# The order and the number in flight of eight weight loads on SyncE's queue, in a state-space mixer followed by an MLP

## The reference

```
x = x + mixer(layernorm(x))
x = x + mlp(layernorm(x))
mixer: proj = h @ W_in * mup; z, xBC, dt = split(proj); xBC = silu(conv4(xBC))
       dt = softplus(dt + bias); dA = exp(dt * -exp(A_log))
       state = state * dA + (dt * x) B;  y = state C + D * x
       g = y * silu(z); g = g * rsqrt(mean(g^2)) * norm_w; out = g @ W_out
mlp:   down(silu(gate(h) * gate_s) * (up(h) * up_s)) * down_s, 512 -> 1408 -> 512
```

## Time and profile before

| what | value |
|---|---|
| time before, median of 3 runs | 766.48 us |
| the three runs | 766.48, 765.35, 768.88 us |
| the profiled execution, its own time | 770.17 us |
| its span, first to last instruction | 768.5 us |
| mean granted TensorE clock | 0.99 |
| PE busy | 735.6 us, 96% of the span |
| DVE, ACT, POOL busy | 513.3, 492.6, 292.2 us |

### The profile page before, as it was taken

The page is one execution under the profiler, slowest core; times in us unless marked ns, Lnnn a source line. Parts: engine busy times, 40 slices in busy tenths (PEclk is TensorE's granted clock), DMA queues, the critical chain, the costliest instruction groups (busy, mean ns, idle before and its releaser), DMA issues.

```text
span 768.5 us, 20313 instructions
## 1 busy us (share of the span) xinstructions
PE 735.6 (96%) x8486; PEld 609.4 (79%) x8486; DVE 513.3 (67%) x845; ACT 492.6 (64%) x933; POOL 292.2 (38%) x235
## 2 busy tenths in 40 slices
PE   4878999999999999999999998989999999999997
PEld 4866778888887887887887886778888888888886
DVE  5977876987987897797797796763624532632331
ACT  6998978978978978979879878624312321321330
POOL 2055276366456547637617707630021011002002
PEclk9988999999999999999999999999999999999999
DMA  9831444484485286366376389535122013002002
GB/s 296 241 93 28 95 112 112 99 243 126 85 243 139 81 210 170 84 160 202 84 210 191 81 227 312 189 99 163 42 70 96 0 42 123 0 16 94 0 1 85
DMA packets 42300, 94.97 MB, mean 124 GB/s; under 512 B 9889, under 2 KB 15777, under 8 KB 42017
## 3 DMA queue, kind: packets, MB, share of 16 engines
q1 hardware_dynamic: 42208, 93.67, 42.8%
HBM read 84.73 MB, written 17.57 MB: 133 GB/s over the span
## 4 chain that ended last, share of the span: by engine, by line
PE 84%; ACT 8%; DVE 4%; issue 2%; DMA 1%; POOL 0%; SPq 0%; ACTq 0%; DVEq 0%; POOLq 0%
PE ps_y L1742 10%; PE ps_proj L1729 10%; PE ps_proj L1271 8%; PE ps_proj L1272 8%; PE ps_proj L1273 8%; PE ps_out L1729 6%; PE ps_x L1729 6%; PE ps_y L1347 5%; PE ps_x L1358 4%; PE ps_out L1371 4%; PE ps_out L1372 3%; PE ps_out L1373 3%; PE ps_x L1324 3%; ACT ring L721 2%; ACT ring L725 2%
## 5 line engine op out<-in xcount | busy, mean ns | idle before, releaser
L532 POOL TENSOR_TENSOR ring<-tokd,ring 128x1024 f32<-128x1024 f32 x64 | 122.3, 1926 | 175.7 <-ACT tokd L716 130.9
L1271 PE MATMUL ps_proj<-xn_hi,win_x_hi 128*128 128x256 f32 x352 | 104.6, 297 | 4.8 <-ACT cin L667 2.9
L1272 PE MATMUL ps_proj<-xn_lo,win_x_hi 128*128 128x256 f32 x352 | 100.2, 285 | 0.0
L1273 PE MATMUL ps_proj<-xn_hi,win_x_lo 128*128 128x256 f32 x352 | 99.9, 284 | 0.0
L962 DVE SCALAR_TENSOR_TENSOR cx<-cin,consts,cx 128x256 f32<-128x256 f32 x240 | 96.3, 477 | 0.0
L1017 DVE TENSOR_TENSOR ring<-ring,ps_tok 128x1024 f32<-128x1024 f32 x64 | 76.0, 1216 | 14.1 <-ACT ring L725 14.0
L1598 POOL TENSOR_TENSOR res<-res,hidden 128x512 f32<-128x512 f32 (+1 forms) x16 | 20.1, 1258 | 166.3 <-DVE hidden L1661 165.3
L1271 PEld LDWEIGHTS ps_proj<-xn_hi,win_x_hi 128*128 128x128 f32 x352 | 67.6, 192 | 18.0 <-issue 8.3
L1271 PE MATMUL ps_proj<-xn_hi,win_z_hi 128*128 128x256 f32 x256 | 74.6, 291 | 0.2 <-ACT sz L664 0.2
L1272 PE MATMUL ps_proj<-xn_lo,win_z_hi 128*128 128x256 f32 x256 | 72.8, 284 | 0.0
L1273 PE MATMUL ps_proj<-xn_hi,win_z_lo 128*128 128x256 f32 x256 | 72.6, 284 | 0.0
(11 more groups left out here) (186 smaller groups left out, 1876.9 us busy)
## 6 DMA issues: line engine op xcount, KB each, us to landing
ring<-cum_dram SPq DMA_DIRECT2D x128, 256.0 KB, 4.8
xin<-x SPq DMA_DIRECT2D x8, 512.0 KB, 3.9
res<-x SPq DMA_DIRECT2D x32, 128.0 KB, 2.8
x_dram<-res SPq DMA_DIRECT2D x32, 128.0 KB, 2.4
res<-x_dram SPq DMA_DIRECT2D x16, 256.0 KB, 2.6
out<-res SPq DMA_DIRECT2D x15, 256.0 KB, 2.0
x_in_sb<-x_dram SPq DMA_DIRECT2D x3, 1024.0 KB, 5.6
gate_w_copy<-gate_w SPq DMA_DIRECT2D x4, 704.0 KB, 6.4
```

What stands on the lines that cost most here:

```text
L532: pool.tensor_tensor(ring[:, g, :, :], own, ring[:, g, :, :], ALU.subtract).then_inc(diffed, 1)
L1271: pe.matmul(out, hi[:, k, :], xn_hi[:, k, :], start=(k == 0), stop=False)
L1272: pe.matmul(out, hi[:, k, :], xn_lo[:, k, :], start=False, stop=False)
L1273: made = pe.matmul(out, lo[:, k, :], xn_hi[:, k, :], start=False, stop=(k == KT - 1))
```

## The change

`load_weights(n)` now waits for part n - 1 where it waited for part n - 2, and part 1 waits too. Parts 4 and 5 move in SP's queue: from ahead of all four tables of step 15 to between the second and the third of them.

```
             def load_weights(n):
 
-                if n >= 2:
-                    sp.wait_ge(hand.weights_in[n % 2], 16 * (n // 2))
+                if n >= 1:
+                    sp.wait_ge(hand.weights_in[(n - 1) % 2], 16 * ((n + 1) // 2))
...
                     else:
                         sp.dma_start(xin[:], hand.x1_by_block[0, :, 0:2, :]).then_inc(hand.first_in, 16)
-                        load_weights(4)
-                        load_weights(5)
...
                 for g in range(GROUPS):
                     load_cums(i, 1, g)
+                    if last and g == 1:
+                        load_weights(4)
+                        load_weights(5)
```

## The result

The changed kernel takes 773.83 us (median of 7 runs, 771.89 to 774.92), the kernel before 766.48 us (763.41 to 769.70) beside it. The ratio on record, which need not be that of the two medians, is 1.0083, 95% interval 1.0062 to 1.0105: slower by 0.83%, some 6.4 us (the medians are 7.3 us apart). The forecast was 765.8 us, and the range up to 769.4 does not hold the result. The profiled execution took 772.99 us, its span 771.2 us (before: 770.17 and 768.5).

A forecast was written before the change was run, and what follows sets the result against it. PE, busy 96% of the span, was taken as the bound, with a 3.57 us stall at step 14. Terms: -3.57 for the stall, +2.87 at the third table, 0 for the rest: -0.7 us, giving 765.8 us, range 763.2 to 769.4.

The forecast's parts named there:

- part (4): Parts 4 and 5 ahead of the third table: it lands at 491.8, ACT clamps at 493.7, gain 0.7 us.
- 0 for the rest: In the sum, everything besides the stall and the third table was taken to cost nothing.
- the 3.57 us of the stall: PE's standstill ahead of the update of step 14, read as a held instruction fetch; nearly all expected to go.
- Part (2): MLP rows issued at 473.4, not 466.61, cost DVE's statistics 1.0 us; POOL's first difference at 482.6; called hidden.
- the timed runs have no such stall: Rival: no stall to gain in timed runs, third table's lateness costs 2.8 us, 769.3 us; chance 0.15.
- The table is not late: Rival: part 4 overtakes the tables' bytes, third table lands at 489.3, gain 3.2 us, 763.3 us; chance 0.15.
- The fetch comes late all the same: Rival: PE's chain and the third clamp stay as before, no change, 766.5 us; chance 0.12.
- The tail is late: Rival: at the end of SP's queue the residual lands beyond 511.5, MLP starts 1 to 2 us later, 768 us; chance 0.08.

The follow-up runs named there:

- The two moves of scale and square: Changed kernel with POOL's scale of step 13 ahead of the third difference and ACT's square of step 14 ahead of the third clamp: 770.61 us, ratio 1.0043.
- The one that takes the parts out of the tables' way: Kernel before, two parts in flight, with weight parts 4 to 7 behind all four tables of step 15: 767.07 us, ratio 1.0001.
- the two other kernels with the same order up to there: Kernel before with only POOL's scale moved (768.03 us, ratio 0.9999), and with only a wait added ahead of the third table (773.30 us, ratio 1.0082).
- the run with parts 6 and 7 together: Changed kernel with weight parts 6 and 7 waiting as before, two in flight: 773.11 us, ratio 1.0073.
- the kernel without weights: Kernel before with all eight weight parts behind the last step's tables, so none move during step 14: profiled span 771.3 us.

## Why the prediction was wrong

**What held.** SP's side of the sum: by the block's clock the MLP rows went at 473.3 (forecast 473.4), part 4 at 477.9 (477.5) with 8.8 us to landing (7 or more), and POOL did wait for the third table. The queue served in order gave the right sequence of landings, each 1.5 to 2 us too early: the MLP rows landed at 480.6 (478.7, 7.3 us from issue and not 5.3), part 4 at 486.7 (485.2), the third table at 493.7 (491.8). The raw times look closer (POOL began the third difference at 492.38, ACT the third clamp at 494.32), but that is the execution's head start of 1.36 us and no merit of the sum.

**The step that failed** is in part (4): "The fourth table follows in the queue ... Hidden, with 0.2 us left", and with it the sum's "0 for the rest". I followed the late table to ACT's clamp and to the fourth difference, and used POOL's scale between them only as 0.73 us of POOL's time. I did not ask who waits for the scale. DVE does (line 1053), and on DVE PE. In the kernel before POOL had it done at 493.57 and DVE used it at 494.35, PE started at 495.24; there was under 1 us of slack. In the changed kernel PE was ready at 491.58, by the block's clock 2.2 us earlier than before, and stood until 496.04. The two moves of scale and square give back about half of the loss in the timed runs; the kernel before with only a late third table (1.0082) shows that such a table is enough to slow it.

**Two terms had the wrong size.** ACT's third clamp came at 495.7 by the block's clock and not at 493.7: 1.25 us later than in the kernel before, not 0.7 us earlier. And of the 3.57 us of the stall PE had won only 2.2 when it came to the product, since a stall of 1.35 us stayed and a gap of 1.24 us opened behind it. By ACT's clamp alone the sum would have been about +1.25 us and not -0.7, the right sign and still within the stated range; for the rest it lacks the scale and what PE's wait for it drew behind it.

**Part (2) was not hidden either.** POOL's first difference came at 484.6 by the block's clock and not at 482.6, and ACT reached `gate_hi(14)` only behind the second clamp, which waited for POOL. In the second profile PE waits 2.0 us for ACT's `keep_tok(15)` by this path.

**A term was missing**: TensorE's clock. The first half of the product took 5.5 us at half clock where it took 2.9. A lower clock follows the stall in the kernel before as well, 0.51 over the 3.4 us behind it. From the update to the third group PE took 6.2 us there and 4.7 us in the changed kernel, so the stall, too, cost more than its 3.57 us:

```profile
479.40:482.80 3.40, 3.40 (x27) 2.67 (x25) 2.52 (x4) 0.38 (x1) 0.00 (x0) 0.51 0.23 59
```

What the clock is worth in the end could not be separated.

**The gain was set too high.** No version won the 3.57 us in the timed runs. The one that takes the parts out of the tables' way, and had only 0.4 us of stall in its profile, is at 1.0001. I had the case that the timed runs have no such stall as a rival, at 0.15. But the profile of the kernel before again had 2.9 us at 767.95 us, and the two other kernels with the same order up to there 1.9 and 1.2 us; so the stall is in some executions at least, and why its removal gains nothing is open. The rival's price of 2.8 us was too low because it, too, went by ACT's clamp alone.

**The other rivals.** "The table is not late" is out: POOL waited 5.4 us and 5.8. "The fetch comes late all the same" is half true: two of the ten profiles with one in flight show it (3.2 and 3.5 us), and in the changed kernel's first profile the gaps without a releaser add up to as much as before. Whether a fetch waits for a part in flight or only for a packet, no run tells apart. "The tail is late" is out by the run with parts 6 and 7 together.

**Open.** Why the gap ahead of the update of step 14 is 0.4 us in one execution and 3.5 in another; how much of the loss is clock and how much the gaps of step 15, which moved whenever instructions were added; and why the run with the late table alone lost 6 us in the timed runs but some 2 us of the block in its profile.

## What to carry to other kernels

When a transfer becomes late, list everything that stands behind its consumer on that engine, also what has nothing to do with the transfer, and for each ask who waits: here a 0.7 us scale behind a late difference held PE for 4.5 us. A wait for one's own predecessor in a DMA queue written in program order holds back every later transfer, so urgent small ones go ahead of bulk (here that was no faster than the kernel before, but it made the rule harmless). Before two profiles are compared, or one with a forecast, bring them to a common point: here 1.36 us of head start made a missed landing look like a hit. A gap in a profile is a gain only if the timed runs improve when it goes.

## What the runs showed of the hardware

After PE stood still for some 4.5 us (3.6 us in the kernel with the late table alone, 2.7 us in the one with two in flight and the new place) its granted clock was 0.50 over the next 5.5 us (0.63 over 4.6 us, 0.52 over 3.5 us). With 18 matmuls in that wait it was 1.00, with 12 of them and 2.1 us still to wait it was 0.53. After the gap of 2.1 us in the last groups of the kernel with 18 matmuls it stayed at 1.00.

A packet of 0.02 MB of the instruction queue q8, which I take for PE's, moves nine times between 444 and 512 us of either profile. Most of the nine leave no gap, but some are followed by one in which PE stands without a releaser: 0.4 to 3.6 us ahead of the update of step 14, 1.3 us among the last groups of the changed kernel, 2.1 to 2.2 us there when 18 or 12 matmuls had been added in front. That these gaps are late fetches is my reading; the profile does not name them. The weights' traffic alone does not explain them: the kernel without weights still has 0.5 us ahead of the update, and in the kernel before the gap of 1.4 us from 503.4 falls in a stretch in which the DMA engines were busy 6% of the time. The Trainium skill (Runtime: NRT & Kernel Launch, "Instruction fetch mechanics") calls this crossing mostly hidden; by number most are, but the ones that are not cost PE 5.0 us in step 14 and 15 of the kernel before.
